# Down halves one chunk later, a new order of the first chunks, and the last experts added on TensorE, in a feed-forward kernel on one core

## The reference, cut to what matters

```python
w = weights[conditions]                            # 128 batches, each a 32 x 32 matrix out of 200
hs = jnp.einsum('bct,bcd->bdt', x, w)              # x: 128 x 32 x 256, float32
logits = jnp.einsum('bsh,he->bse', hs, gate_w)     # 8 experts
routing_weights, _ = jax.lax.top_k(logits, 2)
h = jnp.square(jax.nn.relu(jnp.einsum('bsh,hi->bsi', hs, up_w)))     # 256 -> 1024
y = jnp.einsum('bsi,ih->bsh', h, down_w)                              # 1024 -> 256
y = y + jnp.einsum('bsh,hd->bsd', hs, expert_weight) * routing_weights.sum(-1, keepdims=True)
mu = y.mean(-1, keepdims=True); var = jnp.mean(jnp.square(y - mu), -1, keepdims=True)
out = x + (y - mu) * jax.lax.rsqrt(var + 1e-5) * ln_gamma + ln_beta
```

## Time and profile before

| | us |
|---|---|
| median of 3 runs | 232.68 |
| lowest and highest run | 231.88, 232.74 |
| the profiled execution | 231.9 |
| its span, first to last instruction | 230.2 |
| TensorE busy | 222.6 (97%) |
| VectorE, GpSimd, ScalarE busy | 149.3, 133.5, 107.0 |
| mean granted TensorE clock | 0.995 of full speed |

### The profile page before, as it was taken

One profiled execution on the slowest core, in us unless ns is written; L12 is line 12 of the kernel. 1 busy time (PEld: TensorE's weight loads), 2 busy tenths in 40 slices (PEclk: granted clock), 3 DMA queues, 4 the chain that ended last, 5 costly groups with the idle time before them and its releaser, 6 DMA issues.

```text
span 230.2 us, 3997 instructions
## 1 busy us (share of the span) xinstructions
PE 222.6 (97%) x1264; PEld 191.6 (83%) x1264; DVE 149.3 (65%) x380; ACT 107.0 (46%) x188; POOL 133.5 (58%) x130
## 2 busy tenths in 40 slices
PE   7899999999999999999999999999999999999991
PEld 2697888888888888888888888888888888888991
DVE  6385865666565666766656665656567666666885
ACT  2397945444435444444463444354444444444100
POOL 3729973657546665477536575466653675466422
PEclk9999999999999999999999999999999999999998
DMA  5783313030503020000200002000200002000111
GB/s 187 215 240 122 86 23 101 8 98 7 187 8 98 8 91 5 0 0 3 91 0 3 0 0 94 3 0 0 77 17 0 1 0 95 0 0 0 57 59 68
DMA packets 16889, 11.81 MB, mean 51 GB/s; under 512 B 6628, under 2 KB 16356, under 8 KB 16868
## 3 DMA queue, kind: packets, MB, share of 16 engines
q1 hardware_dynamic: 15140, 9.91, 14.4%
q10 hardware_dynamic: 1312, 1.59, 2.2%
q0 software_dynamic: 416, 0.05, 0.2%
HBM read 7.35 MB, written 4.19 MB: 50 GB/s over the span
## 4 chain that ended last, share of the span: by engine, by line
PE 89%; DVE 3%; issue 2%; DMA 2%; POOL 1%; POOLq 1%; ACT 1%; DVEq 0%
PE up_ps L304 36%; PE down_ps L390 25%; PE down_ps L392 13%; PE hid_ps L277 5%; PE moe_ps L406 3%; PE moe_ps L408 3%; PE moe_ps L407 3%; DMA wd<-in_L_cond_weights_dram 1%; POOL sq_lo L619 1%; POOLq L188 1%; DVE square L511 1%; DVE up_lo L566 1%; DMA cond_row<-in_itok_B_dram 1%; ACT up_hi L455 0%; PE down_ps L277 0%
## 5 line engine op out<-in xcount | busy, mean ns | idle before, releaser
L619 POOL TENSOR_TENSOR sq_lo<-square,sq_hi 128x512 fp32r<-128x512 f32 x64 | 83.8, 1313 | 61.8 <-DVE square L511 61.8
L390 PE MATMUL down_ps<-down_hl,sq_hi 128*128 128x512 f32 x248 | 88.7, 392 | 0.0
L392 PE MATMUL down_ps<-down_hl,sq_lo 128*128 128x256 f32 x248 | 69.6, 280 | 0.0
L511 DVE SCALAR_TENSOR_TENSOR square<-up_ps,relu 128x512 f32<-128x512 f32 x64 | 44.0, 688 | 35.9 <-ACT relu L449 34.7
L390 PEld LDWEIGHTS down_ps<-down_hl,sq_hi 128*128 128x128 f32 x248 | 46.5, 188 | 10.6
L449 ACT ACTIVATE relu<-up_ps 128x512 f32<-128x512 f32 x64 | 38.1, 596 | 32.7 <-PE up_ps L304 32.7
L304 PE MATMUL up_ps<-hid_hi,up_hi 128*128 128x512 f32 (+1 forms) x136 | 53.0, 393 | 0.1
L304 PE MATMUL up_ps<-hid_hi,up_lo 128*128 128x512 f32 (+1 forms) x136 | 51.1, 379 | 0.0
L392 PEld LDWEIGHTS down_ps<-down_hl,sq_lo 128*128 128x128 f32 x248 | 46.7, 188 | 2.4
L451 ACT ACTIVATE sq_hi<-relu 128x512 fp32r<-128x512 f32 x64 | 40.6, 634 | 2.0
L304 PE MATMUL up_ps<-hid_lo,up_hi 128*128 128x512 f32 (+1 forms) x136 | 40.2, 380 | 0.0
(11 more groups left out here) (51 smaller groups left out, 202.8 us busy)
## 6 DMA issues: line engine op xcount, KB each, us to landing
x_sb<-in_x_dram SPq DMA_DIRECT2D x7, 512.0 KB, 3.9
out_dram<-result SPq DMA_DIRECT2D x7, 512.0 KB, 3.0
wd<-in_L_cond_weights_dram SPq DMA_DIRECT2D x110, 4.0 KB, 1.6
result<-in_L_ffn_up_w_dram ACTq DMA_DIRECT2D x2, 512.0 KB, 4.3
x_sb<-in_L_ffn_down_w_dram SPq DMA_DIRECT2D x2, 512.0 KB, 4.9
x_sb<-in_x_dram ACTq DMA_DIRECT2D x1, 512.0 KB, 3.6
out_dram<-result SPq DMA_DIRECT2D x4, 128.0 KB, 1.7
eg_raw<-L_ffn_expert_weight_dram SPq DMA_DIRECT2D x1, 256.0 KB, 3.8
```

Source lines behind the costliest of these rows:

```text
L390: pe.matmul(dst[:, :], a_hi, down_hl[:, c, :, :].rearrange("p s t -> p (s t)"), start=(c == 0), stop=False)
L392: mm = pe.matmul(dst[:, T:2 * T], a_lo, down_hl[:, c, 0, :], start=False, stop=(c == CH - 1))
L511: dve.scalar_tensor_tensor(square[:, c % 2, :], up_ps[c % UPB][:, :], 0.0, relu[:, c % 2, :], ALU.max, ALU.mult).then_inc(square_done, 1)
L619: pool.tensor_tensor(sq_lo[:, j % 2, c, :], square[:, c % 2, :], sq_hi[:, j % 2, c, :].bitcast(f32), ALU.subtract).then_inc(sq_lo_done, 1)
```

## The change

1. **Down halves.** `downs_at` puts each half one chunk later; a block's eighth half goes to chunk 0 of the step after. The last step has nine halves. `total`, `moments`, `inverse_std` and `finish` move along (`tiles_at`).
2. **Opening transfers.** The eight squares of the first half of block 0 are issued by SP (4) and ACT (4), the other eight by POOL (5, which now waits for both loads of `cond_row`) and SP (3, behind a second reading of its list). `x` of block 0 is loaded in two halves, the up weights in three parts, the third of 512 KB by SP ahead of the expert weights and of the down weights.
3. **Opening order.** TensorE takes rests earlier; ACT and VectorE split the second part of up behind the first half's `hidden_first`; VectorE makes `up_hi` of the third part itself. The conditioning of block 1 stands behind chunks 4 and 5.
4. **Down split.** Part 0 is done wholly by POOL (a copy and a subtraction, `split_down_first`) ahead of its first `sq_lo`; part 1 by ACT and VectorE behind chunk 4.
5. **End.** For the very last tile the scaled experts are written as hi and lo and added by two matmuls of 256 columns with an identity; `bn_stats` and the centring read PSUM, and the addition on VectorE goes. The identity is made of `ones` by one instruction on POOL in block 7.
6. **Beta.** POOL adds beta to `x` of block 0 in step 1, chunks 0 and 1, in place of block 0.

The core of the diff:

```diff
-SPLIT_DOWN_AT = {5: 2, 7: 3}
+SPLIT_DOWN_AT = {4: 1, 5: 2, 7: 3}
+BY_SP, BY_ACT, BY_POOL, BY_SP_LATER = range(0, 8, 2), range(1, 8, 2), range(8, 13), range(13, 16)
         def round_at(j):
-            return (4, 6) if j == 0 else (2, 4)
+            return (4, 5) if j == 0 else (2, 4)
+        def downs_at(j, c):
+            order = [(t, half) for t in range(TILES) for half in range(2)]
+            late = [(j - 2, *order[-1])] if j > 1 and c == 0 else []
+            if j == BLOCKS:
+                return late + [(j - 1, *order[c])]
+            return late if c == 0 or j == 0 else [(j - 1, *order[c - 1])]
...
             for b, value in values:
-                sp.dma_start(square_of(b), weights_of(value)).then_inc(wd_first_hw[b // HALF_BLOCK], 16)
+                sp.dma_start(square_of(b), weights_of(value)).then_inc(wd_first_landed[b // Q], 16)
+            values = conditions(mybir.EngineType.SP, BY_SP_LATER)
+            for b, value in values:
+                sp.dma_start(square_of(b), weights_of(value)).then_inc(wd_later_landed[0], 16)
+            load_up(sp, 2)
             sp.dma_start(eg_raw[:, :, 0:T], expert_w.rearrange("(k p) h -> p k h", p=P)).then_inc(eg_landed, 16)
...
+                pe.wait_ge(x_first_landed[half], 16)
+                if half == 0:
+                    pe.wait_ge(wd_first_landed[0], 16 * Q)
+                    condition(0, 0, 0)
+                    condition(0, 1, 0)
+                    pe.wait_ge(wd_first_landed[1], 16 * Q)
+                    condition(0, 0, 1).then_inc(hid_done, 1)
+                    condition(0, 1, 1).then_inc(hid_done, 1)
...
             def first_chunks():
                 conditioning_first(0)
-                for c in range(FIRST - 1):
-                    first_rounded(c, 0)
+                first_rounded(0, 0)
+                first_rounded(1, 0)
+                first_rest(0, 0)
+                first_rest(1, 0)
+                first_rounded(2, 0)
                 conditioning_first(1)
-                first_rounded(FIRST - 1, 0)
-                for c in range(FIRST):
-                    first_rest(c, 0)
+                first_rest(2, 0)
+                first_rounded(3, 0)
+                first_rest(3, 0)
...
+                if last_tile(j, t) and half == 0:
+                    pe.wait_ge(identity_ready, 1)
+                    pe.wait_ge(moe_rest_done, 1)
+                    for part in range(2):
+                        pe.matmul(dst[:, 0:T], identity[:, :], moe_hl[:, part, :], start=(part == 0), stop=False)
...
             act.activation(eg_hi[:, :, :], eg_raw[:, :, :], ACT.Copy).then_inc(eg_hi_ready, 1)
-            split_down(0)
-            split_down(1)
...
             dve.memset(wd[:, TILES:GROUPS, :], 0.0).then_inc(wd_zeroed[1], 1)
+            dve.memset(ones[:, :], 1.0).then_inc(ones_ready, 1)
             split_up(0)
+            hidden_first(0, 0)
+            hidden_first(0, 1)
             split_up(1)
-            for half in range(2):
-                for k in range(K):
-                    hidden_first(half, k)
+            dve.wait_ge(up_landed[2], 16)
+            dve.tensor_copy(up_hi[:, :, split_cols(2)], up_raw[:, :, split_cols(2)]).then_inc(up_hi_ready, 1)
+            hidden_first(1, 0)
+            hidden_first(1, 1)
             split_up(2)
...
+            def split_down_first():
+                pool.wait_ge(down_landed[0], 16)
+                pool.tensor_copy(down_hl[:, down_chunks(0), 0, :], down_raw[:, down_chunks(0), :]) \
+                    .then_inc(down_first_hi, 1)
+                pool.wait_ge(down_first_hi, 1)
+                pool.tensor_tensor(down_hl[:, down_chunks(0), 1, :], down_raw[:, down_chunks(0), :],
+                                   down_hl[:, down_chunks(0), 0, :].bitcast(f32), ALU.subtract) \
+                    .then_inc(down_first_ready, 1)
```

More of the change, by code:

```diff
@@ L83, in adaln_ffn @@
         moe = sb("moe", [P, 2, TILES, T])
+        moe_hl = sb("moe_hl", [P, 2, T], f32r)
+        ones = sb("ones", [P, P])
+        identity = sb("identity", [P, P], f32r)
         y_half = sb("y_half", [P, T])
@@ L174, in experts_at, with tiles_at @@
             return [(j, c // 2)] if j < BLOCKS and c % 2 == 1 else []
+        def downs_at(j, c):
[4 more added lines that the diff above has]
+            return late if c == 0 or j == 0 else [(j - 1, *order[c - 1])]
+        def tiles_at(j, c):
+            return [(block, t) for block, t, half in downs_at(j, c) if half == 1]
         def scaled_at(j, c):
@@ L191, in conditions @@
             return list(zip(batches, values))
[L194 to L201, removed]
         def square_of(batch):
@@ L209, in weights_of, with load_up, load_x_first @@
             return cond_w[bass.ds(row, 1), :, :].rearrange("s c d -> (s c) d")
+        def load_up(queue, part):
+            cols = split_cols(part)
+            queue.dma_start(up_raw[:, :, cols], up_rows[:, :, cols]).then_inc(up_landed[part], 16)
+        def load_x_first(queue, half):
+            part = slice(TILES // 2 * half, TILES // 2 * (half + 1))
+            queue.dma_start(x_sb[:, part, :], x_rows[:, part, :]).then_inc(x_first_landed[half], 16)
         block = ctx.enter_context(nc.Block())
@@ L385, in down @@
                     if last_tile(j, t):
-                        pe.matmul(dst[:, 0:T], a_hi, down_hl[:, c, 0, :], start=(c == 0), stop=False)
+                        pe.matmul(dst[:, 0:T], a_hi, down_hl[:, c, 0, :], start=False, stop=False)
                         pe.matmul(dst[:, 0:T], a_hi, down_hl[:, c, 1, :], start=False, stop=False)
@@ L419, in _ @@
                         up(j, c)
-                    if j > 0:
-                        down(j - 1, c // 2, c % 2)
+                    for block, t, half in downs_at(j, c):
+                        down(block, t, half)
                     for block, t in experts_at(j, c):
@@ L453, in split_up @@
             def split_up(part):
-                act.wait_ge(up_landed[part // 2], 16)
+                act.wait_ge(up_landed[part], 16)
                 act.activation(up_hi[:, :, split_cols(part)], up_raw[:, :, split_cols(part)], ACT.Copy) \
@@ L653, in _ @@
                         split_square(j, c)
-                    if j < BLOCKS and c in (CH - 4, CH - 2):
+                    if j == 1 and c in (0, 1):
+                        add_beta(0, c)
+                    if 0 < j < BLOCKS and c in (CH - 4, CH - 2):
                         add_beta(j, (c - CH + 4) // 2)
-                    if j > 0 and c % 2 == 1:
-                        inverse_std(j - 1, c // 2)
+                    if j == BLOCKS - 1 and c == CH - 1:
+                        pool.wait_ge(ones_ready, 1)
+                        pool.affine_select(identity[:, :], ones[:, :], pattern=[[-1, P]], compare_op=ALU.is_equal,
+                                           fill=0.0, base=0, channel_multiplier=1).then_inc(identity_ready, 1)
+                    for block, t in tiles_at(j, c):
+                        inverse_std(block, t)
 _INS = ["x", "itok_B_1_198", "L0_cond_weights", "L0_ffn_gate_w", "L0_ffn_up_w", "L0_ffn_down_w",
```

121 lines of the change are left out of this document (65 added, 56 removed).

## The result

The changed kernel took 237.01 us (median of 4 runs, 235.06 to 238.20) against 232.28 (4 runs, 231.88 to 232.74) for the kernel before on the same chip: ratio 1.0208, 95% interval 1.0178 to 1.0238. It is slower, as forecast, but by 4.7 us and not by 2.8. The profiled execution took 236.94 with a span of 235.3; before, 231.9 and 230.2, so the spans differ by 5.1.

What follows compares the result with a forecast made beforehand. TensorE was taken to bound the kernel, full in the middle, with gaps only before 27 us and after the last matmul. +3.05 before up(1,1), including the owed half, and -0.2 at the end gave +2.8: 235.5 us, range 232.9 to 237.0.

Steps and rivals of the forecast that it cites:

- down load lands: Opening: the first down load, issued 1.7 us later at 9.3, lands 4.4 to 5.4 us on; 14.2 taken.
- copy on GpSimd: GpSimd's 128x512 copy for the down split, ahead of its first sq_lo: 0.9 us, between 0.61 and 1.29.
- X: Start of GpSimd's first sq_lo, which sets round 1 of block 1's conditioning: 16.8 us, ends 15.4 and 17.9; before, 16.48.
- the exclusion: VectorE's two-input subtraction and GpSimd's sq_lo exclude each other, delaying hid_lo: round 1 at X + 8.0, without it X + 7.2.
- one half still owed: At up(1,1) TensorE still owes one down half, 1.39 us, which step 8 pays as its ninth.
- TensorE behind it: From round 1 of block 1's conditioning to up(1,1): 0.92 + 5.71 + 0.25 us, up(1,1) at 31.7, 1.67 later.
- a stand of 2 to 3 us: Sign: TensorE idle 2 to 3 us before round 1 of block 1's conditioning, near 24.8; under 1 us means wrong.
- the 0.4 for the port: Ahead of GpSimd's first sq_lo: a stop of 0.4 us for the shared SBUF port, moving X from 16.4 to 16.8.
- the light queue: Rival at the opening: down lands before 13, copy cheap, X = 15.4, no exclusion; +0.4, 233.1 us; chance 0.14.
- the closing gaps: Rival before 27 us: round 1 of block 1's conditioning no longer waits, stops close; -1.8, 230.9 us; chance 0.08.
- The third up part: Rival at the opening: its 512 KB load lands late, 13.3, X = 18.3; +1.5 more, 237.0 us; chance 0.12.
- The middle: Rival in the middle blocks: a late square stops TensorE 0.3 us or more per block; +2, 237.5 us; chance 0.04.

Runs made afterwards that it cites:

- part 1 behind `hidden`: Changed kernel with down part 1's split moved from behind chunk 4 to behind `hidden` of round 0, on ScalarE and VectorE: 233.91 us, ratio 1.0084.
- the early squares: Changed kernel with GpSimd issuing its five squares after the first load of the list, waiting for the second load only behind them: 236.61 us, ratio 1.0217.
- its repetition: The changed kernel once more, unedited, six runs: 235.86 us, ratio 1.0159.
- added matmuls: Changed kernel with twelve or six further matmuls of 512 columns, useless for the result, ahead of round 1 of block 1's conditioning: 235.22 us (twelve), 235.28 us (six).
- both back: Changed kernel with round 1 of block 1's conditioning behind chunk 6 again and down part 1's split behind `hidden` of round 0: 233.76 us, ratio 1.0081.
- the kernel at 230.61: Kernel before with the new end, no down split ahead of the main loop (parts behind chunks 3, 5, 7), block 0's beta in step 1: 230.61 us, ratio 0.9942.
- the order put back: Changed kernel with round 1 of block 1's conditioning behind chunk 6 again, no longer behind chunk 5: 233.95 us, ratio 1.0098.
- six fillers: Changed kernel with six added matmuls of 512 columns, useless for the result, ahead of round 1 of block 1's conditioning: 235.28 us, ratio 1.0146.
- the kernel before with the new order: Kernel before with round 1 of block 1's conditioning behind chunk 5: 233.41 us, ratio 1.0077.

## Why the prediction was right in direction and wrong in size

Its steps, in its own order:

| step | forecast | measured |
|---|---|---|
| first product of block 0 earlier by | 0.4 to 0.8 | 9.19 - 8.52 = 0.67 |
| second half of block 0 | 0.6 earlier | about 1 later, 11.77 (off the path) |
| third up part lands | 11.6 | 11.85 |
| down load lands | 14.2 | 15.13 |
| copy on GpSimd | 0.9 | 0.87 |
| X | 16.8 | 17.33 |
| X to square of chunk 3, scaling, square of chunk 4 | 2.60, 1.05, 1.00 | 2.62, 1.06, 0.99 |
| from there to round 1, with the exclusion | 3.37 | 3.24 |
| round 1 | X + 8.0 = 24.8 | X + 7.91 = 25.24 |
| round 1 to up(1,1) | 0.92 + 5.71 + 0.25 = 6.88 | 8.59 |
| one half still owed | 1.39 | first half after up(1,1), at 35.22 |
| middle block | 26.9, full | 26.90 of 26.90 |
| end | -0.2 | -0.3 (alone) |

On the waits the mechanism held: the cause of the stand, its releaser, the exclusion of VectorE's and GpSimd's subtractions, the half that is owed. **The step that failed is "TensorE behind it"**, which took the 5.71 us from round 1's product to up(1,1) over from the earlier trace rows as if TensorE came out of a wait of 2 to 3 us at the pace at which it went in. It didn't: with the lower clock the stretch took 33.83 - 26.16 = 7.67. The same stretch took 6.12 in the kernel with part 1 behind `hidden` and 31.95 - 25.82 = 6.13 in the one with the early squares, which stood 2.72 us as well, both with the clock kept. That is 1.55 us for the clock and 0.16 over the 5.96 forecast. With 0.44 for the later round 1 this is 2.15, and the forecast's increase of 2.8 and the measured 5.1 of the spans differ by 2.3. The prediction named a stand of 2 to 3 us among its signs and gave it no price beyond itself; neither a term nor a rival had the clock in it. The kernels whose traces show the 2.7 us stand (4 executions of the first result, 6 of its repetition, 5 with the early squares) lost the clock in 10 of 15.

With the clock kept the kernel costs +2.9 by its median, which the sum gave at +2.8. That it is so near is in part luck, since the traced executions were later at X and behind it than forecast; the three traces that kept the clock over this order of chunks (two with added matmuls, one with the early squares) have spans of 233.8, 233.8 and 233.4, 3.2 to 3.6 above the 230.2 before.

What could have told: the earlier trace rows have 1.00 as the granted clock, and no stretch of that trace has both a full TensorE behind it and a stand of this length, so no row could say that the stand would cost the clock. What a slow matmul costs did stand there, in a row that neither the rows above nor the prediction use, of the 16 warm-up matmuls ahead of the first work (shortest, median, longest ns):

```profile
L414 PE MATMUL up_ps<-warm x16: 379/634/634, 1.6 to 7.1; 128*128 128x512 bf16 x16
```

0.63 us is what one of 512 columns takes behind the stand too, against 0.38 to 0.39 elsewhere. The granted clock reads 1.00 over the warm-up all the same (in 3 to 6 us of that trace, for one), so whether those were at the lower level is not shown; the distance of the starts is the safer reading.

The Trainium skill names the effect ("TensorE: Matmul & The Clock Gate", section "HAM oscillation — how this bites in real kernels"): idle gaps between bursts of matmuls put the clock back to its lower level, and the time at that level comes on top of the gap. The traces agree, with the addition that it hit 10 of 15 executions here and spared 5; the gaps of the section's example are longer than this one. It had to stand in the prediction as a rival.

The rest of the miss is small, and partly cancels. The down load landed at 15.13, 0.9 later than the middle taken, 5.9 us after its issue at 9.18, past the upper bound of 5.4; why, no run shows. Against that, the copy and the 0.4 for the port were too dear. The forecast has 0.9 + 0.4; measured is 0.87 for both. In the kernel with the early squares the copy takes 0.61, with no VectorE instruction of two SBUF inputs beside it, nearer to the 0.55 that the prediction set against its own price; here it ends 0.48 behind the end of eg_lo (14.82 + 0.70 = 15.52), so 0.26 of its 0.87 was waiting. So the table's 0.9 against 0.87 agrees by luck, and X came only 0.5 late. The second half of block 0 came late for a reason that stands in the change itself: GpSimd waits for both loads of `cond_row` and issues from 5.42 in place of 4.25, while the forecast took its times over from the kernel before. The number of 235.5 also stood on the median of three runs; from the profiled execution it would have been 234.7, so that the anchor hid 0.8 of the gap.

The rivals: the light queue (down before 13) and the closing gaps are out, with X = 17.33. The third up part was not late, and TensorE doesn't stop for it. The middle didn't open.

The kept-clock +2.9 splits, by the single edits: +1.1 for the halves one chunk later, -0.3 for the end, +1.0 for round 1 ahead of chunk 6 with part 1 ahead of `hid_lo` (234.8 less 233.8 with both back), and what is left, 1.1, for the opening and the down split on GpSimd. The last is a difference, not an experiment of its own; X, 0.85 later than before, and VectorE's full list behind it speak for it.

## What to carry to other kernels

When an edit makes TensorE stand for two or three microseconds in an otherwise full stretch, give the stand a second price: what the lower clock costs behind it, as a rival with its own chance, since it may come in some executions and not in others; read it from the granted clock by stretch and from the distance of the starts, never from the busy time. Where an engine's list has no idle row, moving an item within it mostly moves the wait (of 1.37 us, 0.58 came through here), and what helps is to take the item out of the crowded stretch, as the kernel at 230.61 does. A consumer that waits anyway, moved ahead of other work on the full engine (round 1 ahead of chunk 6), gains nothing and loses the work that covered its wait.

## What was not expected of the hardware

- The clock falls not in the stand but behind it: 1.00 from 22.40 to 26.20, then 0.53 and 0.50 until 29.60, and back at 0.97. In another execution, of the unedited repetition, it fell later and came back later:

```profile
26.20:27.00 0.80, 0.80 (x5) 0.67 (x4) 0.80 (x1) 0.80 (x2) 0.80 (x1) 0.72 0.04 6
27.00:28.00 1.00, 1.00 (x4) 0.72 (x4) 1.00 (x2) 0.03 (x1) 0.06 (x1) 0.50 0.06 8
28.00:29.60 1.60, 1.60 (x5) 1.29 (x4) 0.56 (x2) 0.95 (x2) 0.00 (x0) 0.50 0.57 138
29.60:30.60 1.00, 1.00 (x5) 0.81 (x4) 0.34 (x1) 0.28 (x1) 0.58 (x1) 0.82 0.89 309
```

- Stands of 1.2 to 1.4 us (the order put back, part 1 behind `hidden`, six fillers) lost it in none of 14 executions; the 1.37 us stand in the kernel before with the new order came with one of six at a mean clock of 0.991. That this one was the stand's doing was not traced.
- The exclusion also meets GpSimd's copy, which has one input. Beside VectorE's eg_lo (two inputs in SBUF, 0.70 us by itself) it took 0.71, 0.75, 0.84, 0.87 and 1.15 us in five traces and ended 0.47 to 0.48 behind the end of eg_lo in each; where eg_lo was over, or within 0.15 us of its end, 0.61 and 0.62. Where the copy came first (15.02, the kernel with six added matmuls), it took 0.66 and eg_lo 1.12.
- And it meets VectorE instructions with two SBUF inputs of another kind. Centring a tile on VectorE, groups of instructions (busy us, mean ns), after the change:

```profile
L595 DVE SCALAR_TENSOR_TENSOR y<-y,meanvar,gamma_b 128x256 f32<-128x256 f32 x31 | 24.7, 797 | 0.0
```

  and before, 474 ns on the mean for the same instruction. With the halves one chunk later, centring falls beside GpSimd's beta: VectorE's busy time in a middle block rises from 17.3 to 18.9 us, and so it does in the kernel before with the late halves alone (785 ns, 18.9 us). TensorE lost nothing by it there, since its waits lie a chunk or more away.
